# A graph network on one core: edges also ordered by source half, and 272 of the edge gathers issued inside the attention pass

## The reference

```python
# layer 0, three rounds
agg = segment_sum((h @ weight[i])[src], dst);  h = gru_cell(agg, h, ...)
# layer 1: the adjacency is used twice, with weights 1/B and 1/D
# layer 2 (attention)
e = leaky_relu(s1[src] + s2[dst]);  attn = softmax of e over the edges of one src
out = relu(segment_sum(attn[:, None] * mapped[dst], src))
# layer 3 (edge network)
e_in = concatenate([x[src], x[dst]], axis=-1)
edge_new = relu(e_in @ We1 + be1) @ We2 + be2
agg = segment_sum(edge_new, dst)
mesh_new = relu(concatenate([x, agg], axis=-1) @ Wn1 + bn1) @ Wn2 + bn2
x = x + mesh_new
```

## Time and profile before

| | |
|---|---|
| median of 3 runs | 4900.07 us (4892.35 to 4909.78) |
| span of the profiled execution | 4903.2 us; no other time of that execution is shown, so the span stands for it |
| PE busy | 3940.1 us (80%) |
| DVE busy | 3229.5 us (66%) |
| ACT busy | 2297.3 us (47%) |
| POOL busy | 1699.6 us (35%): 856.0 gathers of the edge pass, 808.6 scatters of setup |
| mean granted clock of TensorE | 0.872 of full speed; 0.71 in the edge pass |
| DMA | 858.33 MB, mean 175 GB/s |

### The profile page before, as it was taken

How to read it: one execution, slowest core, us unless ns; L and a number is a source line. 1 busy time by engine, 2 the same in 40 slices (tenths; PEclk the granted TensorE clock), 3 DMA queues, 4 the chain that set the end, 5 groups by cost and what they waited for, 6 DMA issues and landing times. The chain is left out here.

```text
span 4903.2 us, 80623 instructions
## 1 busy us (share of the span) xinstructions
PE 3940.1 (80%) x23797; PEld 3318.4 (68%) x23798; DVE 3229.5 (66%) x7676; ACT 2297.3 (47%) x3163; POOL 1699.6 (35%) x1769
## 2 busy tenths in 40 slices
PE   5888269968899989969989978999995666666557
PEld 3665158746677778747867857999995566665555
DVE  7877669858788878786653356788775444444443
ACT  0001146535555555445555557888763333333333
POOL 3777777774000000000000000000006777777772
PEclk8998689979999999989989988999997666667887
DMA  9910079968288378718878832455433333333331
GB/s 372 355 41 3 1 248 370 325 211 306 70 279 289 115 236 299 243 41 287 294 192 288 294 115 62 142 147 147 143 106 114 103 103 103 103 103 103 103 103 46
DMA packets 318859, 858.33 MB, mean 175 GB/s; under 512 B 84767, under 2 KB 109073, under 8 KB 318603
## 3 DMA queue, kind: packets, MB, share of 16 engines
q1 hardware_dynamic: 205964, 619.48, 38.7%
q10 hardware_dynamic: 57185, 177.25, 9.6%
q0 software_dynamic: 55456, 58.46, 4.8%
HBM read 669.98 MB, written 185.03 MB: 174 GB/s over the span
## 5 line engine op out<-in xcount | busy, mean ns | idle before, releaser
L925 POOL DMA_INDIRECT big<-table,idx_ring x880 | 856.0, 973 | 2780.5 <-ACT idx_ring L943 2512.7
L1433 POOL DMA_INDIRECT adj_t<-cell_val,cell_at x832 | 808.6, 972 | 321.6 <-issue 321.6
L765 PE MATMUL ps<-tiles_r,stage_r 128*128 128x512 f32 x2028 | 806.5, 398 | 30.8 <-ACT tiles_r L714 24.8
L991 PE MATMUL ps<-big,stage 128*128 x1760 | 403.3, 422 | 315.1 <-DVE onehot L1003 157.9
L991 PEld LDWEIGHTS ps<-big,stage 128*128 128x128 f32 x1760 | 374.6, 324 | 336.7 <-issue 336.6
L635 DVE TENSOR_SCALAR_CACHE_REDUCE big<-ps 128x512 f16<-128x512 f16 (+2 forms) x724 | 429.4, 652 | 123.1 <-PE ps L587 111.8
L714 ACT CAST tiles_r<-onehot 128x1024 fp32r<-128x1024 f16 x338 | 354.9, 1050 | 289.5 <-PE ps L767 143.2
L772 PE MATMUL ps<-stage,big 128*128 128x130 f32 x4046 | 467.6, 278 | 18.9 <-DVE big L875 15.8
L965 ACT ACTIVATE stage<-stage 128x512 f32<-128x512 f32 x220 | 138.4, 629 | 729.5 <-DVE stage L1018 729.5
L772 PEld LDWEIGHTS ps<-stage,big 128*128 128x128 f32 x4046 | 463.3, 194 | 19.6 <-issue 15.8
L765 PEld LDWEIGHTS ps<-tiles_r,stage_r 128*128 128x128 f32 x2028 | 386.2, 190 | 124.4 <-issue 25.9
(11 more groups left out here) (429 smaller groups left out, 7601.9 us busy)
## 6 DMA issues: line engine op xcount, KB each, us to landing
onehot<-adj_t SPq DMA_DIRECT2D x332, 512.0 KB
big<-adj_t SPq DMA_DIRECT2D x332, 512.0 KB
onehot<-adj_s SPq DMA_DIRECT2D x170, 512.0 KB
adj_t<-rows ACTq DMA_DIRECT2D x13, 6656.0 KB
adj_s<-big ACTq DMA_DIRECT2D x157, 512.0 KB
stage<-local_rows SPq DMA_DIRECT2D x110, 512.0 KB, 3.8
big<-adj_s SPq DMA_DIRECT2D x84, 512.0 KB
x_fm<-adj_s SPq DMA_DIRECT2D x84, 512.0 KB
```

Of the source, the lines that this page charges most:

```text
L765: nc.tensor.matmul(psum_fm(p, n)[:, 0:cut], upper_rows[:, k, :], tile[:, 0:cut], start=k == 0, stop=False, skip_group_check=True)
L925: nc.gpsimd.indirect_dma_start(row_ring[slot][:, u, :], None, table[0:N, :], bass.IndirectOffsetOnAxis(idx_ring[:, slot * CH + u:slot * CH ...
L991: last = nc.tensor.matmul(ps[:, 4 + 2 * h + g, (u % 4) * P:(u % 4 + 1) * P], ring_ohT[:, h * CH + u, :], q_nm[:, bass.ds(blk[u] * P, P)], ...
L1433: nc.gpsimd.indirect_dma_start(out, bass.IndirectOffsetOnAxis(cells[:, c:c + 1], 0), cell_val[:, c:c + 1], None).then_inc(S(name), 16)
```

## The change

Edges are ordered a second time, by whether their source is below node 2048 (`LATE_FROM`, four groups of 512) or not, and by destination within each half. A tile is now 128 edges of one block of one half: 98 block counts in place of 49 and 928 tiles in place of 880. The second ordering is 832 more indirect DMAs on POOL, of single values to `edges_halves`; they stand behind the scatters of the matrix. The tiles' edges are fetched after pass 3 (8 indirect DMAs), and the arithmetic, transposes and copies of `local` and `gather_idx` are done within the first group of pass 4.

In the attention pass each finished group is transposed on PE, copied by ACT, multiplied by the first half of `We1`, copied and stored to `table` by SP, two groups behind. The four PSUM banks of a group become two, so that two are free for this. After five stored groups (nodes 6144 and up, then 0 to 2047) POOL may gather for the first 272 tiles; it gathers 16 tiles at a time into `x_fm` and stores them, with a DMA of its own queue, to `early_rows` in DRAM, 17 times. The x3 stage no longer makes `P`; it waits at chunk 10 for the last of these stores, as it writes where they are read.

The edge pass has 116 chunks: 34 early ones, loaded by SP, and 82 with gathers (656), in turns of six (`DEDDED`, E early, D with gathers; 17 turns, then 14 of D). POOL's 656 gathers are written out without a loop and take their indices from `gather_idx`. The one-hots have three buffers in place of four, and 3 chunks' worth of degrees are loaded ahead in place of 10.

```diff
+HALVES = 2
+VB = HALVES * NB
+T = -(-((E + VB * (P - 1)) // P) // (2 * CH)) * 2 * CH
+RANKS = 5
+LATE_FROM = (RANKS - 1) * GW
+EARLY = 34
+EARLY_PAIRS = EARLY // 2
+DIRECT = CHUNKS - EARLY
+TURN = "DEDDED"
-DEGREES_EARLY = 10
+DEGREES_EARLY = 3
...
+            def x3_kept(q, g):
+                act.wait_ge(S("x3_flipped"), q + 1)
+                nc.scalar.copy(x_nm[:, bass.ds(g * KT, KT), :].rearrange("p b f -> p (b f)"), att_rows).then_inc(S("x3_kept"), 1)
+                wait(act, S("p_given"), q)
+                nc.scalar.copy(x3_cols, x3_turned).then_inc(S("x3_kept"), 1)
+
+            def p_kept(q):
+                act.wait_ge(S("p_given"), q + 1)
+                wait(act, table_stored, 16 * q)
+                nc.scalar.copy(p_rows, p_sums).then_inc(S("p_kept"), 1)
...
         def psum_nm(p, n, m):
-            return ps[:, 4 * ((groups_before(p) + n) % 2) + m, 0:AW]
+            at = 2 * ((groups_before(p) + n) % 2) + m // 2
+            return ps[:, at, m % 2 * AW:m % 2 * AW + AW]
...
+                    if mode == "att" and n > 0 and t == 10:
+                        x3_flips(n - 1 + LOOPED * i)
+                    if mode == "att" and t == 1 and behind_two(n, i):
+                        p_products(n - 2 + LOOPED * i)
+
+            def x3_flips(q):
+                pe.wait_ge(S("att_steps"), ATT_STEPS * q + ATT_STEPS)
+                for b in range(KT):
+                    last = nc.tensor.transpose(x3_turned[:, b * P:(b + 1) * P], att_rows[:, b * P:(b + 1) * P], ident[:, :])
+                last.then_inc(S("x3_flipped"), 1)
...
+            for k in range(EARLY_PAIRS):
+                pool.wait_ge(table_stored.sem, pool.value_load(early_need[0:1, k:k + 1], min_val=table_stored.base + 16 * RANKS,
+                                                               max_val=table_stored.base + 16 * GROUPS))
...
+                for u in range(2 * CH):
+                    if u == CH // 2 and k > 0:
+                        store(k - 1)
+                    gather(pool, early_ring[2 * (k % 2) + u // CH][:, u % CH * P:(u % CH + 1) * P], 2 * CH * k + u
+                           ).then_inc(early_in[k % 2], 16)
+            store(EARLY_PAIRS - 1)
...
+            for k in range(DIRECT):
+                slot = k % HOT
+                if k >= HOT:
+                    pool.wait_ge(S("edge_pre"), 2 * direct_at(k - HOT) + 2)
                 for u in range(CH):
+                    gather(pool, row_ring[slot][:, u, :], (EARLY + k) * CH + u).then_inc(half_landed[2 * slot + u // 4], 16)
...
+            for n in range(SL):
+                for c in range(SLW):
+                    if n and c == SC:
+                        sorted_there(n - 1)
+                    at = n * SLW + c
+                    nc.gpsimd.indirect_dma_start(edges_halves, bass.IndirectOffsetOnAxis(slot_at[:, at:at + 1], 0),
+                                                 slot_val[:, at:at + 1], None).then_inc(halves_written[n % 2].sem, 16)
+            sorted_there(SL - 1)
+            pool.wait_ge(stage_end, ended["third"])
...
-            turns(dve, (NB + 1) // 2, count_block)
+            turns(dve, VB // 2, count_block)
...
             for c in range(REAL_CHUNKS):
                 wait(act, F("flip_done", "_x3"), c + 1)
+                if c == (TW + KT * P) // CN:
+                    wait(act, early_stored, 16 * EARLY_PAIRS)
```

More of the change, by code:

```diff
@@ L459, in gnn, with behind_two, two_back @@
         STEP = LOOPED * TURNS
+        def behind_two(n, i):
+            return n > 0 and not (n == 1 and isinstance(i, int))
+        def two_back(n, g, i):
+            return GROUPS - 1 if isinstance(i, int) and n == 2 else g - 2
         SCALED = 4
@@ new lines, in edge_turns, with turn, direct_at @@
+        def edge_turns(eng, body):
+            def turn(i):
+                for h in range(len(TURN)):
+                    body(Spot(i, h))
+            turn(0)
+            with eng.Fori(1, LOOPS - 1) as i:
+                turn(i)
+            turn(LOOPS - 1)
+            for x in range(1, SPARE + 1):
+                body(Spot(0, 0, x))
+        def direct_at(k):
+            if k >= PER_TURN * LOOPS:
+                return len(TURN) * LOOPS + k - PER_TURN * LOOPS
+            spots = [h for h in range(len(TURN)) if TURN[h] == "D"]
+            return len(TURN) * (k // PER_TURN) + spots[k % PER_TURN]
@@ L962, in body @@
+            def body(spot):
+                h = spot.par
+                if not spot.last:
+                    turned_hots(spot.after())
                 for g in range(2):
                     pre = ring_e[:, h * CH + 4 * g:h * CH + 4 * g + 4, :].rearrange("p t e -> p (t e)")
-                    wait(act, S("edge_pre"), 2 * c + g + 1)
+                    wait(act, S("edge_pre"), 2 * spot.u + g + 1)
                     nc.scalar.activation(pre, pre, ACT.Relu).then_inc(S("edge_act"), 1)
-                if at is None or at + HOT < CHUNKS:
-                    for g in range(2):
-                        wait(act, half_landed[2 * slot + g], 64 * (use + 1))
-                    indices(c + HOT, slot)
@@ L994, in body, with hots @@
                     last.then_inc(S("q_given"), 1)
-                if at != 0:
-                    sums_of(c - 1, (slot - 1) % HOT)
+                if not spot.first:
+                    sums_of(spot.before())
+                if spot.last:
+                    sums_of(spot)
             edge_turns(pe, body)
-            sums_of(CHUNKS - 1, (CHUNKS - 1) % HOT)
         def edge_dve(dve):
-            def hots(c, slot):
+            def hots(spot):
                 nc.vector.tensor_tensor(
-                    hot_ring[slot],
+                    hot_ring[spot.hot],
@@ L1030, in body @@
-            def body(c, slot, use, at):
-                if at != CHUNKS - 1:
-                    hots(c + 1, (slot + 1) % HOT)
-                if at != 0:
-                    blk = tile_blocks(dve, c - 1)
-                gathered(c, slot, use)
-                if at != 0:
-                    adds_of(c - 1, 1 - slot % 2, blk)
+                    wait(dve, S("added"), CH * spot.u + u)
+                    nc.vector.tensor_tensor(dst, psum_sum(spot.par, u, P), dst, ALU.add).then_inc(S("added"), 1)
@@ L1038, in edge_dve, with body @@
+            def body(spot):
+                if not spot.last:
+                    hots(spot.after())
+                if not spot.first:
+                    blk = tile_blocks(dve, spot.before().chunk)
+                gathered(spot)
+                if not spot.first:
+                    adds_of(spot.before(), blk)
+                if spot.last:
+                    adds_of(spot, tile_blocks(dve, spot.chunk))
             edge_turns(dve, body)
-            adds_of(CHUNKS - 1, (CHUNKS - 1) % 2, tile_blocks(dve, CHUNKS - 1))
@@ L1839, in _ @@
             last.then_inc(S("w_given"), 1)
+            pe.wait_ge(S("w_taken"), 2)
+            pe.wait_ge(S("sums_asked"), 11)
+            nc.tensor.matmul(ps[:, 3, 2 * CN - SL:2 * CN], lower[:, :], extras, start=True, stop=True)
+            nc.tensor.matmul(ps[:, 3, 2 * CN - 2 * SL:2 * CN - SL], ones[:, :], extras, start=True, stop=True)\
+                .then_inc(S("sums_given"), 1)
             def h0_product(c, s):
```

456 lines of the change are left out of this document (297 added, 159 removed).

## The result

| | before | after |
|---|---|---|
| time, median | 4900.43 us (4892.35 to 4909.78) | 4720.23 us (4716.66 to 4730.8) |
| profiled execution | 4903.2 us span | 4721.78 us, span 4720.0 |
| ratio, 95% interval | | 0.9637, 0.962 to 0.9655 |

What follows compares the result with a forecast made beforehand. POOL's gather issue was taken to bound the edge pass, PE the attention pass. The edge pass would end 263 us earlier after all terms: 4903.2 - 263 = 4640 span, 4637 as timed; 8-in-10 range 4600 to 4715.

Steps and rivals of the forecast that it cites:

- The step that failed: Edge pass: 656 direct gathers at 1.275 us take POOL 836 us from 3710; walked with DVE, 849 us, to 4559.
- Scatters, +5 us: 832 more scatters on POOL under passes 1 to 3: contact with DVE's casts mostly hidden, +5 us, bounds 0 and +50.
- Setup, -9: Setup and first pass: DVE's added work is covered by a wait; 7 pair gathers leave POOL's scatter queue, -9 us.
- Pass 4, +4: Pass 4, bound by PE: the pair work moves here, 3 us of transposes and a gap, +4 us.
- Attention pass, +18.5: Attention pass: PE's added transposes, products and semaphore gaps over 12 groups, +18.5 us; 22 taken for the whole, bounds +12 and +45.
- Early gathers: POOL from 3337: 272 gathers, 347 us, and 17 stores at 1.4 us, 24 us; free for direct gathers at 3710.
- Edge pass, DVE: Edge pass: DVE alone needs 6.92 us a chunk, 116 chunks, 803 us from 3738 to 4541.
- B: Edge pass: PE stays at its lower clock, 7.6 us per chunk, stage ends at 4620, kernel 4698; chance 0.11.
- C: Passes 1 and 2 slow by 5% beside the scatters, 50 us in place of 5, kernel 4682; chance 0.07.
- D: Passes: DVE locks POOL out, scatters at 2.65 us pitch, pass 4 waits, +405, 5042; sign decided from 2.2 us; chance 0.04.
- E: Early gathers need all 13 groups and start at 3683, the edge pass ends at 4904, kernel 4977; chance 0.03.
- F: Edge pass: DVE faster than read, POOL alone bounds, 4631, or 4613 with other low ends; low end of main case (0.72).

Runs made afterwards that it cites:

- a_halves3: The changed kernel with each chunk's one-hot cut into two tensor_tensor instructions of four tiles; 4684.68 us, ratio to the kernel before 0.9572.
- a_e24: The changed kernel with 24 early chunks and not 34; 4763.3 us, ratio to the kernel before 0.9726.

## Why the prediction was wrong

The direction and most steps were right, and the sizes of two terms were off: the direct gathers, and the passes beside the second scatters, which account for most of the late start of the early gathers. Forecast span 4640, measured 4720.0, 80 us: the early gathers began 24 us late, they took 12 us longer, the direct ones 41 us longer, what stands between the last gather and the last add 7 us longer (12.5 for 5), and the tail was 5 us shorter.

- *The step that failed.* "656 x 1.275 = 836", "Walking both chunk by chunk gives 3710 + 849": measured 3746.5 to 4636.5, 890 us. That is 1.357 us a gather for 1.275. The duration of a gather was read as POOL's own, from a stretch where DVE waited on POOL and ran its one-hot mostly at a harmless place. The row that showed otherwise stood in the profile: the earlier trace rows gives a maximum of 1824 ns beside a median of 952, and POOL's mean there, 0.973, is 21 ns above the median; the excess sits in 110 of the 880. The same change that took DVE's wait away took the rhythm away with it. a_halves3 shows the hold's price; that the rhythm made it small is what the two stretches of the changed kernel and of a_e24 show, and the direct trial of it was inconclusive. The second term off is the +5 of the scatters below, 21 us in passes 1 and 2.
- *The rule of the Trainium skill.* The prediction took a sentence on two-port modes from the Trainium skill, "SBUF — State Buffer", section "Who interferes with whom", and set it aside because "none of POOL's was longer for it". That reading was wrong. The earlier trace rows gives 1602 ns at most beside a median of 967, and 26 of the 832 scatters lasted over 980 ns. Two of them, each behind what DVE ran when it started (kernel before; 110.50 is the longest):

```profile
110.34 0.92 DVE L2234 SCALAR_TENSOR_TENSOR big<-acc,big 128x728 f32<-128x728 f32 x1
110.50 1.60 POOL L1433 DMA_INDIRECT adj_t<-cell_val,cell_at  x1 [0.31 <-issue]
...
639.61 0.63 DVE L2384 TENSOR_SCALAR acc<-acc 128x896 int32<-128x896 int32 x1 [5.10 <-DMA acc<-edges,pair_idx]
639.71 1.38 POOL L1433 DMA_INDIRECT adj_t<-cell_val,cell_at  x1 [0.30 <-issue]
```

They end 0.84 and 0.85 us behind the DVE instruction, the hold of the edge pass, and the second of these instructions has one input. On the same list of the Trainium skill stands that a DVE instruction with two SBUF inputs contends with a GpSimd instruction that reads SBUF. By that rule the trace agrees: 115 gathers, which take their indices from SBUF, start inside the one-hot and end 0.826 us behind it in the mean. Where the list infers that a `tensor_tensor` does not stall a DMA, the measurement is against it. The attention pass has holds too: 168 of the 272 early gathers started inside DVE's L1025, which reads two SBUF tiles, and lasted 1128 ns, 29.6 of the 30.0 us that these gathers lost.
- *Scatters, +5 us.* The contact with the casts is there ("at most 0.17 us of each"; measured 0.064), but it was not hidden: the passes grew by 10.7 and 10.1 us, as much as 169 x 0.064, so DVE's idle 17% was no cover. SP's loads wait for the casts, which the prediction left out. Added to the kernel before, such scatters cost 11 to 13 us of its time. They ended at 2269 us, forecast 2255.
- *Setup, -9.* Measured -7 at the end of the first pass (1213.5 against 1220.5). *Pass 4, +4:* +3.4. *Attention pass, +18.5:* 633.8 against 618.6 us, +15. All three right.
- *Early gathers.* 1.062 + 0.31 us each for 1.275: +26 us. The 17 stores, taken at 1.4 us each, took 0.59 us of POOL and little else: -14. The stage behind the attention pass did wait for the last store, as forecast, 40.8 us; the first sum came at 3777, forecast 3741, of which 24 us is the late start.
- *Edge pass, DVE.* 6.87 us a chunk, forecast 6.92: right. In the turns with early chunks POOL's 4 x 11.0 us over 6 chunks make 7.33.
- *Rivals.* B (lower clock): no; PE's q products took 334 ns each in the mean, 422 before, and the granted clock in the edge pass was 0.86 for 0.71. C: in part, 21 us over passes 1 and 2, under half of its 50. D: the contact exists, at 1.016 us a scatter in the mean, with a pitch of 1.32, far from the 2.2 us where it decides the sign. E: no, the early gathers began at 3361 us and not at 3683. F was not reached, since POOL's mean pace was 1.357 and not 1.275.

## What to carry to other kernels

An instruction's duration in a profile belongs to the overlap in which it was taken; look for its maximum and for what ran beside the long ones before multiplying the mean by a new count, above all when the change removes a wait that kept two engines in step. Where GpSimd's DMAs bound a stage, the DVE instructions that hold them, here those from SBUF to SBUF, should be short: cutting the one-hot in two gave 36 us for one line, while replacing it by eight lost 33 on DVE. And price a transfer moved off the critical end by what then becomes late: at 34 chunks, ten early ones gave 43 us for 102 us of gathers.

## What the runs showed of the hardware that was not expected

- A gather on GpSimd that starts while DVE runs a tensor_tensor from two SBUF tiles is held to that instruction's end: 1519 ns in the mean for 952, at most 1982. A tensor_scalar of 128x128 holds it likewise, but lasts 0.28 us and costs it 36 ns in the mean (989). A tensor_tensor of a PSUM and an SBUF input does not (951).
- The other way round a scatter costs an f16 to fp32r cast of 128x1024 64 ns in the mean (754 for 690).
- DVE's register load of eight block numbers (L463 of the changed kernel) lasted 1.84 us, 4211.13 to 4212.97; the one-hot of 1.22 us covers it only in part, and 0.68 of the 1.13 us of "issue" in each chunk lie beside it.
- The kernel before took 4895 us beside some runs and 6118 to 6193 us beside others, on other chips. In the latter condition PE was busy 130 of 1000 us in the changed kernel's first pass beside POOL's scatters; in the kernel before, in the other condition, it was busy 491 of 560 us in this pass, with POOL's scatters beside it too.
